# First attention of a four-layer kernel: Q's second part goes to the other projection bank, TensorE's loop is split by batch, and the last pair projects nothing

## The reference, cut to what matters

```python
def _L0_attn_ref(query, Wq, Wk, Wv, Wp, bp):          # query (2, 1024, 128), Wq/Wk/Wv (16, 128, 64)
    q = jnp.einsum('bnd,hde->bhne', query, Wq) * scale
    k = jnp.einsum('bmd,hde->bhme', query, Wk)
    v = jnp.einsum('bmd,hde->bhme', query, Wv)
    attn = jax.nn.softmax(jnp.einsum('bhne,bhme->bhnm', q, k), axis=-1)
    out = jnp.einsum('bhnm,bhme->bnhe', attn, v)
    out = jnp.swapaxes(out, -1, -2).reshape(B, N, E * H)
    return jnp.dot(out, Wp) + bp
x = _layernorm(x + _L0_attn_ref(x, ...))
```

## Time and profile before

| | us |
|---|---|
| median of three runs | 1187.3 |
| the profiled execution | 1186.8 |
| its span | 1184.8 |
| TensorE matmul busy | 1053.6 (89%) |
| VectorE busy | 894.0 (75%) |
| ScalarE busy | 734.1 (62%) |
| GpSimd busy | 671.6 (57%) |

### The profile page before, as it was taken

One profiled execution on the slowest core, in us unless ns is written; L12 is line 12 of the kernel. 1 busy time (PEld: TensorE's weight loads), 2 busy tenths in 40 slices (PEclk: granted clock), 3 DMA queues, 4 the chain that ended last, 5 costly groups with the idle time before them and its releaser, 6 DMA issues. The chain is left out here.

```text
span 1184.8 us, 25711 instructions
## 1 busy us (share of the span) xinstructions
PE 1053.6 (89%) x7981; PEld 849.6 (72%) x7981; DVE 894.0 (75%) x1768; ACT 734.1 (62%) x1367; POOL 671.6 (57%) x667
## 2 busy tenths in 40 slices
PE   6889999999999999999999998568974898999996
PEld 5678888888888888888888886345853666666664
DVE  5877887787787788788778774666756488899997
ACT  4556666666666666666666665544443777777774
POOL 4266676676676676667667666110320676676772
PEclk9999999999999999999999999798997899999998
DMA  5333534444353353443434330100001202221101
GB/s 117 68 75 75 117 72 100 98 89 96 78 114 81 67 122 73 89 109 77 102 83 103 83 76 4 47 1 1 1 1 39 80 13 65 80 69 53 53 1 36
DMA packets 57720, 80.18 MB, mean 68 GB/s; under 512 B 26515, under 2 KB 38734, under 8 KB 56654
## 3 DMA queue, kind: packets, MB, share of 16 engines
q1 hardware_dynamic: 55478, 79.17, 28.3%
q10 hardware_dynamic: 2208, 0.59, 0.3%
HBM read 19.63 MB, written 1.11 MB: 18 GB/s over the span
## 5 line engine op out<-in xcount | busy, mean ns | idle before, releaser
L596 POOL TENSOR_TENSOR probs_lo<-probs 128x512 f16<-128x512 f32 x384 | 393.8, 1043 | 248.5 <-ACT probs L439 247.3
L460 DVE TENSOR_REDUCE maxes<-bank_m 128x1 f32<-128x512 f32 x512 | 348.9, 689 | 82.6 <-PE bank_m L268 76.1
L439 ACT ACTIVATE probs<-bank_s 128x512 f32<-128x512 f32 x512 | 305.1, 600 | 86.8 <-PE bank_s L356 61.8
L1228 POOL TENSOR_TENSOR hidden_lo<-hidden,hidden_hi 128x512 fp32r<-128x512 f32 x111 | 173.5, 1585 | 92.5 <-ACT hidden_hi L1377 92.2
L349 PE MATMUL bank_s<-qa,ka 128*128 128x512 f32 x512 | 217.8, 425 | 3.0 <-DVE v_parts L507 2.5
L268 PE MATMUL bank_m<-ka,qa 128*128 128x512 f32 x512 | 211.1, 412 | 6.2 <-DMA ka<-tk_lo 3.9
L356 PE MATMUL bank_s<-qb,kb 65*128 65x512 f32 x512 | 205.6, 402 | 1.2 <-DMA qb<-negmax 1.2
L291 PE MATMUL bank_o<-v_now,probs 128*128 128x129 f16 x2048 | 200.6, 220 | 1.4 <-DVE probs_lo L536 1.3
L291 PEld LDWEIGHTS bank_o<-v_now,probs 128*128 128x128 bf16 x2048 | 175.4, 97 | 22.3 <-issue 20.7
L268 PEld LDWEIGHTS bank_m<-ka,qa 128*128 128x128 f32 x512 | 158.6, 310 | 38.5 <-DVE maxes L460 12.6
L287 PE MATMUL bank_o<-v_now,probs_lo 128*128 128x65 f16 x2048 | 184.6, 193 | 0.0
(11 more groups left out here) (226 smaller groups left out, 1591.9 us busy)
## 6 DMA issues: line engine op xcount, KB each, us to landing
qa<-tq_hi SPq DMA_DIRECT2D x64, 256.0 KB, 4.0
v_now<-v_parts SPq DMA_DIRECT2D x32, 260.0 KB, 2.3
ka<-tk_hi SPq DMA_DIRECT2D x32, 256.0 KB, 2.9
ka<-tk_lo SPq DMA_DIRECT2D x32, 256.0 KB, 4.9
kb<-tk_hi SPq DMA_DIRECT2D x32, 256.0 KB, 5.0
qb<-tq_lo SPq DMA_DIRECT2D x32, 256.0 KB, 5.1
gates_on_all<-gate_rows SPq DMA_DIRECT2D x8, 1024.0 KB, 4.7
e_raw<-in_L_ffn_ew_dram SPq DMA_DIRECT2D x16, 256.0 KB, 5.2
```

Source lines behind the costliest of these rows:

```text
L439: nc.scalar.activation(probs[:, c, u, :], bank_s[u % 2][:], ACT.Exp, scale=SCALE).then_inc(exp_done, 1)
L460: nc.vector.tensor_reduce(maxes[:, j // 2, j % 2:j % 2 + 1], bank_m[j % 2][:], AX.X, ALU.max).then_inc(m_reduced, 1)
L596: nc.gpsimd.tensor_tensor(probs_lo[:, c, u, :], p, hi, ALU.subtract).then_inc(lo_pool, 1)
L1228: nc.gpsimd.tensor_tensor(h_lo[:, f, :], h[:, f, :], h_hi[:, f, :].bitcast(F32), ALU.subtract).then_inc(lo_pool, 1)
```

## The change

q1 goes to bank 0; the table `PART_BANK` has the bank of each of the four. The counts of `x_taken` and `x_filled` follow: in a pair, bank 0 is now filled five times (before: four) and bank 1 three times (before: four). So q1 waits until `add_y` of step 0 has freed bank 0, and `turn_o` of step 1 waits for q1's `make_lo`. On TensorE there are two loops, over 6 and 8 turns, one for the projections of each batch, so that the column is a constant. The last turn (steps 2, 3 of pair 14 and 0, 1 of pair 15) is written out on all engines. In it, pair 15 makes no projections, no `take_part`, no `make_lo`, no `load_weights` and no `stage`.

```diff
+    PART_BANK = (1, 0, 1, 1)
...
-        def over_steps(eng, step, before, after):
+        def over_steps(eng, step, before, after, stretches=((0, PAIRS_ALL - 2),)):
+
+            def turn(i, lo):
+                step(i, 2)
+                step(i, 3)
+                step(i + 1, 0, lo=lo)
+                step(i + 1, 1, lo=lo)
...
-            with eng.Fori(0, PAIRS_ALL - 1) as i:
-                step(i, 2)
-                step(i, 3)
-                step(i + 1, 0)
-                step(i + 1, 1)
+            for lo, hi in stretches:
+                with eng.Fori(lo, hi) as i:
+                    turn(i, lo)
+            turn(PAIRS_ALL - 2, PAIRS_ALL - 2)
...
-        x0_base = lambda i: 4 * i - 2
-        x1_base = lambda i: 4 * i + 2
+        x0_base = lambda i: 5 * i - 2
+        x1_base = lambda i: 3 * i + 2
...
+        def part_use(k, i):
+
+            if k == 1:
+                return 2 if isinstance(i, int) and i == 0 else x0_base(i) + 2
+            return x1_base(i) + (0, None, 1, 2)[k]
...
-                    load_weights(i + 2)
+                    if not no_next(i):
+                        load_weights(i + 2)
...
-                col = ((i // PAIRS) % persist["B"]) * N + c * CH
-                out, xs = bank_x[bank][:], bass.ds(col, CH)
+                col = batch * N + c * CH
+                out, xs = bank_x[bank][:], slice(col, col + CH)
...
-                    if (s, u) in PROJECT_AT:
+                    if (s, u) in PROJECT_AT and not no_next(i):
                         w, ch, k = PROJECT_AT[s, u]
-                        project(w, ch, i + 1, 1, x1_base(i) + k)
+                        project(w, ch, i + 1, PART_BANK[k], part_use(k, i), 0 if first else (lo + 2) // PAIRS)
...
-            over_steps(pe, step, before, after)
+            over_steps(pe, step, before, after, [(max(b * PAIRS - 2, 0), (b + 1) * PAIRS - 2) for b in range(B)])
...
-                        take_part(w, ch, 1, x1_base(i) + k + 1)
+                        take_part(w, ch, PART_BANK[k], part_use(k, i) + 1)
...
-                        make_lo(w, ch, 1, 4 * (i + 1) + k, i if k == 0 else None)
+                        make_lo(w, ch, PART_BANK[k], 4 * (i + 1) + k, i if k == 0 else None)
...
-                    if s == 1 and u == UNITS - 1:
-                        pool.wait_ge(x_filled[1], x1_base(i) + 4)
+                    if s == 1 and u == UNITS - 1 and not no_next(i):
+                        pool.wait_ge(x_filled[1], x1_base(i) + 3)
                         stage(i + 2)
```

More of the change, by code:

```diff
@@ L146, in over_steps @@
             after()
+        no_next = lambda i: isinstance(i, int) and i == PAIRS_ALL - 1
         def max_at(i, s, u, first, last):
@@ L154, in max_at, with x0_use @@
             return None if last and h == 1 else (1 - h, 2 * i + h + 1, j)
-        x0_base = lambda i: 4 * i - 2
-        x1_base = lambda i: 4 * i + 2
+        x0_base = lambda i: 5 * i - 2
+        x1_base = lambda i: 3 * i + 2
+        X0_END = x0_base(PAIRS_ALL) - 1
+        def x0_use(i, s):
+            return x0_base(i) + (2 if s and no_next(i) else 3 * s)
+        def part_use(k, i):
+            if k == 1:
+                return 2 if isinstance(i, int) and i == 0 else x0_base(i) + 2
+            return x1_base(i) + (0, None, 1, 2)[k]
         @block.sync
@@ L209, in load_wp @@
                 if not first:
-                    sp.wait_ge(x_taken[0], x0_base(i) + 4)
+                    sp.wait_ge(x_taken[0], X0_END if no_next(i) else x0_base(i) + 5)
                 rows_of = persist["Wp"].rearrange("(e h) o -> h e o", h=H)
@@ L227, in before, with step @@
                 load_v(0, 0)
-            def step(i, s, first=False, last=False):
+            def step(i, s, first=False, last=False, lo=0):
                 if s == 0:
                     load_head(1, i, 0 if first else 32 * i)
-                    load_weights(i + 2)
+                    if not no_next(i):
+                        load_weights(i + 2)
                     load_row(0, 1, 4 * i + 1)
@@ L250, in _, with project @@
         def _(pe):
-            def project(which, c, i, bank, use):
+            def project(which, c, i, bank, use, batch):
                 pe.wait_ge(staged, i + 1)
@@ L323, in before @@
                 for w, c, bank, use in (("q", 0, 1, 0), ("q", 1, 0, 0), ("k", 0, 1, 1), ("k", 1, 0, 1)):
-                    project(w, c, 0, bank, use)
+                    project(w, c, 0, bank, use, 0)
                 pe.wait_ge(xlo_ready, T // 4)
@@ L363, in step @@
                         times_v(pi, psn, PV_TO[u - 1] if u else 0, PV_TO[u])
-                    if (s, u) in PROJECT_AT:
+                    if (s, u) in PROJECT_AT and not no_next(i):
                         w, ch, k = PROJECT_AT[s, u]
-                        project(w, ch, i + 1, 1, x1_base(i) + k)
+                        project(w, ch, i + 1, PART_BANK[k], part_use(k, i), 0 if first else (lo + 2) // PAIRS)
                     if not first and s < 2:
                         if u == OT_AT:
-                            turn_o(i - 1, s, x0_base(i) + 2 * s)
+                            turn_o(i - 1, s, x0_use(i, s))
                         if u == Y_AT:
-                            times_wp(i - 1, s, x0_base(i) + 2 * s + 1)
+                            times_wp(i - 1, s, x0_use(i, s) + 1)
             def after():
@@ L376, in after @@
                 for c in range(2):
-                    turn_o(i - 1, c, x0_base(i) + 2 * c)
-                    times_wp(i - 1, c, x0_base(i) + 2 * c + 1)
-            over_steps(pe, step, before, after)
+                    turn_o(i - 1, c, X0_END + 2 * c)
+                    times_wp(i - 1, c, X0_END + 2 * c + 1)
+            B = persist["B"]
+            over_steps(pe, step, before, after, [(max(b * PAIRS - 2, 0), (b + 1) * PAIRS - 2) for b in range(B)])
         @block.scalar
@@ L429, in step @@
                             take_o(bi, bs, qt)
-                    if (s, u - 1) in PROJECT_AT:
+                    if (s, u - 1) in PROJECT_AT and not no_next(i):
                         w, ch, k = PROJECT_AT[s, u - 1]
@@ L440, in step @@
                     if not first and s < 2 and u == OT_AT + 1:
-                        take_turned(x0_base(i) + 2 * s + 1)
+                        take_turned(x0_use(i, s) + 1)
             def after():
@@ L449, in after @@
                     take_o(i - 1, 3, qt)
-                take_turned(x0_base(i) + 1)
-                take_turned(x0_base(i) + 3)
+                take_turned(X0_END + 1)
+                take_turned(X0_END + 3)
             over_steps(act, step, before, after)
@@ L536, in step @@
                         nc.vector.tensor_tensor(probs_lo[:, c, u, :], p, hi, ALU.subtract).then_inc(lo_dve, 1)
-                    if (s, u - 1) in PROJECT_AT:
+                    if (s, u - 1) in PROJECT_AT and not no_next(i):
                         w, ch, k = PROJECT_AT[s, u - 1]
-                        make_lo(w, ch, 1, 4 * (i + 1) + k, i if k == 0 else None)
+                        make_lo(w, ch, PART_BANK[k], 4 * (i + 1) + k, i if k == 0 else None)
                     if not first and s < 2 and u == Y_AT + 1:
-                        add_y(i - 1, s, x0_base(i) + 2 * s + 2)
+                        add_y(i - 1, s, x0_use(i, s) + 2)
             def after():
@@ L547, in after @@
                 for c in range(2):
-                    add_y(i - 1, c, x0_base(i) + 2 * c + 2)
-                dve.wait_ge(x_taken[0], x0_base(i) + 4)
+                    add_y(i - 1, c, X0_END + 2 * c + 2)
+                dve.wait_ge(x_taken[0], X0_END + 4)
             over_steps(dve, step, before, after)
```

## The result

The changed kernel takes **1176.0 us** (median of four runs, 1175.46 to 1176.36) where the kernel before takes 1188.1 (four runs, 1186.91 to 1189.11). The ratio is 0.990, with a 95% interval of 0.988 to 0.9915: between 10 and 14 us faster. The forecast was 11.4 us and 1175.9.

What follows compares the result with a forecast made beforehand. TensorE's queue was taken to set the pace, held up by waits for VectorE's `make_lo` ahead of projections. Gains 4.9 + 2.3 + 4.25 = 11.45, rounded to 11.4, gave 1187.3 - 11.4 = 1175.9 us; range 1173 to 1181.

Steps and rivals of the forecast that it cites:

- What bounds the kernel: First attention: TensorE sets the pace, held up by 28 waits for `make_lo` ahead of projections, 20.6 us in total.
- q1's wait changes its object and grows by 0.60: Pairs 1 to 14: q1 waits for `add_y` instead of `make_lo`, 0.60 us longer.
- Gain 0.35 us a pair: Pairs 1 to 14: unit behind k0 starts at 279.25, not 279.60; 4.9 us over 14 pairs.
- Pair 0, 2.3 us: Pair 0 has no `add_y`, so both waits go: 5.33 us become 3.04, gain 2.3 us.
- rival 1: Middle pairs gain nothing, for instance through a late reduction; only pairs 0 and 15 gain, 6.5 us: 1180.8; chance 0.14.
- one of my signs of being wrong: Step 1, unit 2: prediction wrong if the third matmul shows a wait for a reduction.
- Pair 15, 4.25 us: Last pair without projections: 4.8 us gained, 0.55 given back for a late third matmul in unit 2, gain 4.25 us.
- Loops at 0 with 0.3 us either way: TensorE's two loops and written-out turn cost 0, with 0.3 us either way for code met first.
- Everything behind lasts what it lasted: Layers behind the first attention move forward as a block, their duration unchanged.
- both waits go: Every pair: q1 finds bank 0 free, no wait at q1 or k0; 2.0 us a pair, 1153 in all; chance 0.03.
- the time won is waited for elsewhere: No difference in total, as pair 0 waits for a row of maxima: 1187; chance 0.05.
- The clock: q1's 1.38 us wait lowers TensorE's clock, costing 1.5 us a pair, 21 us in all: 1197; chance 0.05.

Runs made afterwards that it cites:

- loops alone: Kernel before with TensorE in two loops of 6 and 9 turns and a constant column, nothing else: 1188.8 us, ratio 1.0001.
- last pair alone: Changed kernel with all four projections back in bank 1, last turn still written out without projections in pair 15: 1184.5 us, ratio 0.9966.
- swap alone: Kernel before with q1 in bank 0 and the matching counts, one loop, column from registers, last pair still projecting: 1183.0 us, ratio 0.995.
- both with one loop: Changed kernel with `add_y` ahead of q0's `make_lo`, q1 at (1, 1), TensorE in one loop of 14 turns, column from registers: 1160.2 us.
- two reductions more: Changed kernel with two unused VectorE reductions of 512 columns ahead of `add_y` in step 0 of pairs 1 to 14: 1217.4 us.
- q1 later: Changed kernel with q1 one unit later, at (1, 1) instead of (1, 0): 1167.2 us, ratio 0.9826.
- `add_y` first: Changed kernel with `add_y` ahead of q0's `make_lo` on VectorE in unit 7 of step 0: 1168.1 us, ratio 0.9833.
- both: Changed kernel with `add_y` ahead of q0's `make_lo` and q1 at (1, 1), two loops kept: 1160.7 us, ratio 0.9771.
- short reduction more: Changed kernel with one unused VectorE reduction of 128 columns ahead of `add_y` in step 0 of pairs 1 to 14: 1182.8 us.
- one reduction more: Changed kernel with one unused VectorE reduction of 512 columns ahead of `add_y` in step 0 of pairs 1 to 14: 1206.4 us.

## Why the prediction was right, point by point

- **What bounds the kernel**: right. Every variant's total follows TensorE's waits at q1 and k0, and the clock behind them. The 28 waits of the earlier trace rows are those of pairs 1 to 14; pair 15 has two more behind the end of that view, and the forecast counted them apart, in the earlier trace rows.
- **q1's wait changes its object and grows by 0.60**: right, from 0.78 to 1.37 us. **The wait at k0 goes**: right.
- **Gain 0.35 us a pair**: right in size (0.37), and in part by luck. I took 0.83 us from the start of the releasing operation to q1, and held that the register instructions of the column were not in the way. They were: in the kernel before one of them stands between the release and q1. But in the changed kernel another instruction takes its place, one that does nothing but wait for bank 0, since the instruction behind it waits for the weights. The records of TensorE's own queue show it; medians over the pairs:

| where | freed by | first instruction that waits for the bank | from the start of VectorE's operation to it | to q1's matmul |
|---|---|---|---|---|
| loops alone, last pair alone | `make_lo` | q1's weight load itself | 0.74 | 0.74 |
| before | `make_lo` | a register instruction, then the load | 0.72 | 0.83 |
| pair 0 of the kernel before | `make_lo` | a waiting instruction, then the load | 0.73 | 0.83 |
| changed kernel | `add_y` | a waiting instruction, then the load | 0.72 | 0.82 |
| swap alone, both with one loop | `add_y` | a waiting, a register instruction, then the load | 0.72 | 0.94 |

  In the view of one line, the register instruction of the kernel before (q1 at 318.28 and 360.80) and the waiting instruction of the changed one (q1 at 312.99 and 355.58):

```profile
L258 PEldq FUSED_REGOPS  x3: 51/51/138, 318.2 to 360.7; - x3
```

```profile
L275 PEldq EVENT_SEMAPHORE  x2: 51/51/51, 312.9 to 355.5; - x2
```

  So a release by `add_y` reaches TensorE no later than one by `make_lo`, and each instruction between the release and the weight load costs 0.11 us. The row of pair 0 in the earlier trace rows, on which I leaned, is a good guide for the changed kernel because its q1 has the same two instructions, and not because registers are free. Without the constant column q1 has all three, and the swap gains 0.2 us a pair.
- **Pair 0, 2.3 us**: 1.90. The term that was mis-sized is the two units between q1 and k0, taken at their plain 1.40 us: unit 2's third matmul waits for a reduction, which costs 0.4 us there. It is the thing that rival 1 feared for the middle pairs and I had charged in pair 15 alone; it was also one of my signs of being wrong, and it shows in pairs 0 and 15 only.
- **Pair 15, 4.25 us**: 4.31, with the late third matmul in unit 2 where the earlier trace rows said that it would be (692.11). Not foreseen: the row of maxima is 0.33 us late for step 2. TensorE arrives there 0.7 us sooner after the row's transfer was issued, and the transfer takes longer: 3.5 us from issue to landing, beside a packet of the instruction queue, where the same row took 1.9 in the kernel before. By these times neither alone would have made the wait. From 697 to 701 us in the changed kernel:

```profile
q8 instruction: 1, 0.02, 2.1%
...
qb<-negmax SPq DMA_DIRECT2D x1, 2.0 KB, 3.5
```

  The time came back within the pair, as the table's next place shows.
- **Loops at 0 with 0.3 us either way**: the size was right for the total, and the trace shows 0.4 us once in the changed kernel, at the first turn of the second loop (a pair of 42.56 among pairs of 42.17).
- **Everything behind lasts what it lasted**: wrong by 2 us in the two profiles, and not by the change. From the first instruction of the second layer to the end of the span the twelve kernels, which have the same code there, take:

| kernel | rest, us | kernel | rest, us | kernel | rest, us |
|---|---|---|---|---|---|
| before | 443.2 | loops alone | 446.5 | two reductions more | 444.5 |
| changed | 445.4 | last pair alone | 443.2 | q1 later | 445.7 |
| swap alone | 445.9 | `add_y` first | 444.9 | both | 445.8 |
| both, one loop | 444.5 | short reduction more | 446.9 | one reduction more | 446.8 |

  The spread of 3.7 us has no order by what the kernels do in the first attention; what makes it was not tried. The start of the first attention spreads too (46.7 us in the changed kernel, 48.3 before, 46.9 to 48.4 in others). So of two single profiles the span's difference, 10.5 us, tells less than the difference between places, 11.44.
- **The rivals**: that the trade is worth nothing in the middle (0.14) is refuted by the pair's distance; that both waits go (0.03) too, in this kernel; two further edits made it nearly true, with 0.24 us a pair left. That the time won is waited for elsewhere (0.05) is refuted by the total; what it feared, a late row of maxima, came twice in the changed kernel, with 0.3 us each. The clock was the rival with a real mechanism.

## What to carry to other kernels

When a buffer is swapped to end a wait, find the operation that frees the new one on the same engine: here it stood one place behind the old one, so the swap alone bought 0.2 us a pair, and the order of two operations bought a further 0.6. Move the release forward (`add_y` first) and the demand back (q1 a unit later) before adding buffers: together they took away all but 0.24 us of the wait, for 27 us against 12. When a wait has gone from the list of waits, look at the distance between starts before you call it gone. And treat a repeated wait of TensorE of about 1.5 us as one that may cost double.

## What the runs showed of the hardware

- TensorE's granted clock was 1.00 through 14 waits of about 1.37 us in pairs of 42 us. It fell after 1 of 15 waits of about 1.5 us, 2 of 14 of 1.6, 12 of 14 of 1.7 to 2.0, and 13 of 14 of 2.6. A fall to the 1.2 GHz level costs 1.5 us here, more where it lasts longer. The Trainium skill says in TensorE: Matmul & The Clock Gate, section "A second HAM failure mode: psum-queue depth-cycling", that in one kernel short idle times between groups of matmuls were frequent enough to make the clock swing. The kernels with one and two reductions more agree that short repeated idle times can do it (granted clock 0.97 and 0.96 over the loop), the changed kernel does not yet show it (1.00). All of them have one such wait in each pair, so here it is the length that made the difference.
- A waiting TensorE takes its next step 0.72 to 0.74 us after the start of the 128x512 operation on VectorE that it waits for, and each further instruction ahead of the weight load adds 0.11 us (the table above).
- A row of maxima, a transfer of 2 KB, lands later when a packet of the instruction queue (q8) runs beside it. From 120 us on such packets came only where TensorE met a stretch of code for the first time: in the first turn of its second loop, and behind its last loop. In the changed kernel the transfers of two stretches of 4 us, at the second loop's first turn and a pair earlier, read:

```profile
q8 instruction: 1, 0.02, 1.5%
...
qb<-negmax SPq DMA_DIRECT2D x1, 2.0 KB, 2.4
```

```profile
qb<-negmax SPq DMA_DIRECT2D x1, 2.0 KB, 1.9
```

  The first has a packet of the instruction queue and takes 2.4 us from issue to landing, the second has none and takes 1.9. It is so throughout: from 120 us to the end of the first attention, over all twelve kernels, 33 rows had such a packet start 0.4 to 1.6 us behind their issue, and all 33 took 2.4 to 3.8 us; the other 651 took 1.9 to 2.0, but for two of 2.2. No edit tried to move a packet. Few of the late rows make TensorE wait. At the second loop's first turn the wait was 0.3 us in the changed kernel and 0.28 to 0.98 in five others, and three (`add_y` first, both edits, the short reduction) had none. The Trainium skill, Runtime: NRT & Kernel Launch, section "Instruction fetch mechanics", tells that a branch to code outside the fetched window stalls the engine; here TensorE did not stall at the branch itself, it waited for data that came late. In the changed kernel the matmuls at the second loop's start stand as far apart as those of an earlier pair, within 0.06 us, until the late row.
